# Causal attention of a fused transformer kernel: the order of TensorE's products within a unit, by the way they use the array

## What is computed

```python
q, k, v = x @ w_q[h].T, x @ w_k[h].T, x @ w_v[h].T      # per head h
scores  = q @ k.T / sqrt(64)                            # position i sees j <= i only
out     = concat_h(softmax(scores) @ v) @ w_o.T
x       = x + out
```

## Time and profile before

| | us |
|---|---|
| median of three runs | 2433.93 (2432.94 to 2435.12) |
| the profiled execution | 2433.29 |
| its span, first to last instruction | 2431.4 |
| TensorE busy, matmuls | 2165.6 (89%) |
| VectorE busy | 1550.0 (64%) |
| ScalarE busy | 1035.3 (43%) |
| mean granted TensorE clock | 0.947 of full speed |

### The profile page before, as it was taken

One profiled execution on the slowest core, in us unless ns is written; L12 is line 12 of the kernel. 1 busy time (PEld: TensorE's weight loads), 2 busy tenths in 40 slices (PEclk: granted clock), 3 DMA queues, 4 the chain that ended last, 5 costly groups with the idle time before them and its releaser, 6 DMA issues.

```text
span 2431.4 us, 39297 instructions
## 1 busy us (share of the span) xinstructions
PE 2165.6 (89%) x13553; PEld 1354.2 (56%) x13594; DVE 1550.0 (64%) x4432; ACT 1035.3 (43%) x1761; POOL 145.0 (6%) x271
## 2 busy tenths in 40 slices
PE   4569999996699989999999997999999599998698
PEld 3413333334577756566565665777766367775476
DVE  6798888857534346666666665444456735787776
ACT  2126666672234335555554553433333133343133
POOL 5011111115000000000000000000000000000000
PEclk9679999997799989999999998999999789999899
DMA  6010000000000000000000000000100000000000
GB/s 215 13 65 26 25 25 25 25 11 1 1 1 1 1 1 1 1 0 0 0 0 0 0 1 1 1 1 1 55 1 1 0 1 1 1 1 1 1 1 18
DMA packets 20863, 32.04 MB, mean 13 GB/s; under 512 B 5657, under 2 KB 12194, under 8 KB 19970
## 3 DMA queue, kind: packets, MB, share of 16 engines
q1 hardware_dynamic: 20018, 30.12, 3.6%
q10 hardware_dynamic: 720, 0.27, 0.1%
HBM read 25.80 MB, written 4.19 MB: 12 GB/s over the span
## 4 chain that ended last, share of the span: by engine, by line
PE 63%; DVE 9%; ACT 3%; issue 2%; ACTq 0%; DVEq 0%; POOL 0%; POOLq 0%
PE ps L408 19%; PE ps L393 18%; PE ps L604 6%; PE ps L638 5%; PE ps L621 3%; PE ps L588 3%; DVE x L819 1%; ACT arena L736 1%; PE ps L610 1%; PE ps L334 1%; DVE arena L801 1%; PE ps L901 1%; PE ps L256 1%; PE ps L650 1%; PE ps L1055 1%
## 5 line engine op out<-in xcount | busy, mean ns | idle before, releaser
L408 PEld LDWEIGHTS ps<-l_w,arena 128*128 128x128 f32 x4096 | 543.6, 194 | 262.2 <-issue 246.2
L408 PE MATMUL ps<-l_w,arena 128*128 128x128 f32 x4096 | 546.9, 277 | 12.1 <-DVE x L495 10.2
L393 PE MATMUL ps<-xnT,l_w 128*128 128x512 f32 x1024 | 537.8, 609 | 3.3 <-ACT xnT L264 3.3
L495 DVE SCALAR_TENSOR_TENSOR x<-ps,comb,x 128x128 f32<-128x128 f32 x768 | 216.4, 344 | 376.4 <-PE ps L408 374.5
L451 ACT ACTIVATE arena<-ps,l_b 128x512 f32<-128x512 f32 x384 | 263.6, 687 | 410.9 <-PE ps L393 410.8
L1962 DVE TENSOR_REDUCE arena<-ps 128x1 f32<-128x512 f32 x512 | 325.2, 685 | 34.2 <-PE ps L1747 32.2
L1890 ACT ACTIVATE arena<-ps 128x1024 f32<-128x1024 f32 x256 | 252.3, 1022 | 124.7 <-PE ps L1764 124.2
L801 DVE TENSOR_REDUCE arena<-ps 128x1 f32<-128x128 f32 (+7 forms) x256 | 179.0, 751 | 75.8 <-PE ps L610 74.5
L736 ACT ACTIVATE arena<-ps,arena 128x128 f32<-128x128 f32 (+7 forms) x256 | 186.8, 744 | 72.0 <-DVE arena L801 72.0
L1747 PE MATMUL ps<-arena 128*128 128x512 bf16 x480 | 173.6, 394 | 8.3 <-DVE arena L1962 6.0
L744 ACT ACTIVATE arena<-ps 128x512 f32<-128x512 f32 (+1 forms) x192 | 85.4, 489 | 211.6 <-PE ps L621 211.4
(11 more groups left out here) (319 smaller groups left out, 2036.6 us busy)
## 6 DMA issues: line engine op xcount, KB each, us to landing
arena<-s_parts_q SPq DMA_DIRECT2D x96, 48.0 KB
arena<-s_parts_k SPq DMA_DIRECT2D x96, 48.0 KB
l_w<-in_l_w SPq DMA_DIRECT2D x2, 2048.0 KB, 13.9
l_w<-in_l_w SPq DMA_DIRECT2D x4, 1024.0 KB, 12.3
s_parts_q<-arena SPq DMA_DIRECT2D x2, 768.0 KB, 4.3
s_parts_k<-arena SPq DMA_DIRECT2D x2, 768.0 KB, 5.2
arena<-arena SPq DMA_DIRECT2D x96, 2.0 KB
x<-in_x SPq DMA_DIRECT2D x4, 256.0 KB, 4.2
```

The lines of the kernel that those rows point to most:

```text
L393: pe.matmul(k.ps[:, n % 2, :], w.w1[:, e, f * P:(f + 1) * P], k.xnT[:, g * GW:(g + 1) * GW], start=True, stop=True).then_inc(s.hidden_mm.s ...
L408: ins = pe.matmul(k.ps[:, 2 + e % 4, j * P:(j + 1) * P], w.h[:, n % 2, j * P:(j + 1) * P], w.w2[:, e, f, :], start=(f == 0 and j == 0), st ...
L495: ins = dve.scalar_tensor_tensor(k.x[:, t, :], k.ps[:, 2 + e % 4, j * P:(j + 1) * P], k.comb[:, t, e:e + 1], k.x[:, t, :], ALU.mult, ALU.add)
```

## The change

TensorE's stream. Where there are projections, each unit now has exactly one, and it stands between the two `turn`s; `values` and `output` come after `turn(f, u, 1)`. The k projections move forward from behind `turn(f, u, 1)`. The waits are placed anew: `output` now waits for the copy of k out of bank 7, the q projection of u2 for `y_used` too, the v projection of u4 for `y_used` instead of a `kv_out`. ScalarE: `weights_out` is ahead of the exponentials in u2 too, and `q_copy` goes ahead of `o_copy`. VectorE: `kv_copy` of k moves ahead of `weights_out`, and `add` behind it.

```diff
                 turn(f, u, 0, begin)
+                if not end:
+                    if u == 0:
+                        pe.wait_ge(s.kv_out, 4 * f + 4)
+                        if b == 1:
+                            pe.wait_ge(s.slices, 2 * p + 4)
+                        project("q", 0, p + b, 1 - b, 7)
+                    if u == 1:
+                        pe.wait_ge(s.q_out, 2 * f + 3)
+                        project("k", 0, p + b, 1 - b, 7)
+                    if u == 2:
+                        pe.wait_ge(s.kv_out, 4 * f + 5)
+                        if not begin:
+                            pe.wait_ge(s.y_used, 4 * f - 1)
+                        project("q", 1, p + b, 1 - b, 7)
+                    if u == 3:
+                        pe.wait_ge(s.q_out, 2 * f + 4)
+                        project("k", 1, p + b, 1 - b, 7)
+                    if u == 4:
+                        pe.wait_ge(s.y_used, 4 * f + 1)
+                        project("v", 0, p + b, 1 - b, 7)
+                    if u == 5:
+                        pe.wait_ge(s.kv_out, 4 * f + 7)
+                        project("v", 1, p + b, 1 - b, 7)
+                turn(f, u, 1, begin)
                 if u == 0 and not begin:
                     values(f - 1, 1 - b, (6, 7))
                 if u == 1 and not begin:
-                    if not end:
-                        pe.wait_ge(s.q_out, 2 * f + 3)
+                    pe.wait_ge(s.kv_out, 4 * f + (4 if end else 5))
                     output(2 * f - 1, before)
                 if u == 2:
                     values(f, b, (2, 3), first=begin)
                 if u == 3:
-                    if not end:
-                        pe.wait_ge(s.q_out, 2 * f + 4)
+                    if end:
+                        pe.wait_ge(s.y_used, 4 * f - 1)
+                    else:
+                        pe.wait_ge(s.kv_out, 4 * f + 6)
                     output(2 * f, p)
                 if u == 4:
                     values(f, b, (4, 5))
-                if u == 0 and not end:
...
-                turn(f, u, 1, begin)
-                if u == 1 and not end:
-                    if begin:
-                        pe.wait_ge(s.q_out, 2 * f + 3)
-                    else:
-                        pe.wait_ge(s.y_used, 4 * f - 1)
-                    project("k", 0, p + b, 1 - b, 7)
-                if u == 3 and not end:
-                    pe.wait_ge(s.y_used, 4 * f + 1)
-                    project("k", 1, p + b, 1 - b, 7)
```

More of the change, by code:

```diff
@@ L757, in pair @@
             for u in range(U):
-                if u != 2:
-                    weights_out(f, u)
+                weights_out(f, u)
                 if u < U - 1:
@@ L763, in pair @@
                     exp(f + 1, 1 - b, 0)
-                if u == 2:
-                    weights_out(f, u)
+                if u in (0, 2) and not end:
+                    q_copy(f + 1, 1 - b, u // 2, 7)
                 if u == 0 and not begin:
@@ L769, in pair @@
                     o_copy(2 * f)
-                if u in (0, 2) and not end:
-                    q_copy(f + 1, 1 - b, u // 2, 7)
     q_copy(0, 0, 0, 2)
@@ L830, in pair @@
                     negmax(f + 1, 0)
+                if u in (4, 5) and not end:
+                    kv_copy("v", f + 1, 1 - b, u - 4, 7)
+                if u in (1, 3) and not end:
+                    kv_copy("k", f + 1, 1 - b, u // 2, 7)
+                weights_out(f, u)
                 if u == 1 and not begin:
@@ L834, in pair @@
                     add(f * 2, b * TB)
[L835 to L839, removed]
     for bank, what, g in ((3, "k", 0), (5, "k", 1), (6, "v", 0), (7, "v", 1)):
```

## The result

The changed kernel took 2423.0 us (median of 5 runs, 2418.4 to 2423.5), the kernel before 2433.9. The ratio is 0.9944, with a 95% interval of 0.9928 to 0.996: faster by 0.56%. The forecast was 2415.5, the range 2408 to 2426: right in sign and inside the range, with 11 us gained where 18.4 were forecast.

A forecast was written before the change was run, and what follows sets the result against it. TensorE's stream was taken as the bound. Per pass -1.30 - 1.79 + 1.80 = -1.3 us; fifteen passes -19.5, last pass +1.1, so 2433.9 - 18.4 = 2415.5 us, range 2408 to 2426.

The forecast's parts named there:

- What bounds: In a 37.6 us pass TensorE, busy 35.8 us, is the bound; only time leaving its stream shortens the pass.
- The changes removed: Seven of TensorE's 24 changes of array use per pass go, at 0.15 or 0.20 us each: 1.30 us saved.
- my first rival: At TensorE's removed changes of use, weight loads stay exposed, so the gain is only 6 us: 2428 us; chance 0.06.
- The waits removed: The k projections in u1 and u3 stop waiting for the addition to empty bank 7, and lose entries: 1.79 us.
- The waits added: TensorE waits for VectorE before u1's output, u2's values and u3's output: 2.10 us, or 1.80 net of exits.
- What stays at nothing: ScalarE's copies between the turns and its exponentials stay covered, with slack of about 0.1 and 0.4 us: no added wait.
- The last pass: Without projections, turns stand back to back in u0 to u4: 2.2 us lost, 1.1 saved on changes, so +1.1.
- The sum: Each pass 1.3 us shorter; fifteen passes -19.5, last pass +1.1: -18.4 us in all.
- its two unknowns: Scores' entry after output costing nothing (+6 us), and u2's VectorE chain off by 0.4 us either way (6 us).
- Rival 2: Before u2's values, VectorE's late addition delays TensorE one for one; taking twice its 2.59 us gives 2455 us; chance 0.05.

The follow-up runs named there:

- even units: The kernel before, with TensorE's new order in u0, u2 and u4 only and ScalarE's new order: 2428.3 us, ratio 0.9968.
- exchange of banks: The changed kernel with head 0's output in bank 6 and head 1's in bank 7, waits adjusted to match: 2405.7 us, 0.9876 of before.
- second timing: The unaltered changed kernel timed again against the kernel before, beside variants: 2422.4 us against 2435.7, ratio 0.9945.
- odd-units kernel: The changed kernel with TensorE's old order in u0, u2 and u4 and ScalarE's stream as before: 2429.3 us, ratio 0.9973.
- last-pass kernel: The changed kernel with values and output back between the two turns in the last pass alone: 2429.0 us, one execution.

## Why the prediction was right, and what it mis-sized

- *What bounds.* TensorE's stream, at a granted clock of 1.00 through the block. Every change to it showed in the time, pass by pass.
- *The changes removed, 1.30 us.* Right. The even units alone gave 0.58 for three (0.60 forecast); the other four, 0.70, were not timed by themselves, but the rows agree: a projection behind whole-array work takes 0.86 us, its pitch alone, and scores behind the output pay no entry (1.39 us against 1.49), the one that no row of before showed. The rule on which my first rival rested ("TensorE: Matmul & The Clock Gate", section "What overlaps and what doesn't", in the Trainium skill) did not decide here: projections of 128 rows behind transpositions of 128 rows went in 0.86 us, with no weight load in the open.
- *The waits removed, 1.79 us.* Right: no wait and no entry is left at line 588.
- *The waits added, 2.10 us.* This is the term that was mis-sized. By starts less pitch they are 0.19 (I said 0.17), 1.37 (1.2) and 0.71 or, in every other pass, 0.88 (0.73): 2.36 in the mean. With their exits taken off, 2.07 instead of 1.80. Of the 0.27, 0.18 is that the late semaphore was asked ahead of others in the loop: 0.10 in u2, and 0.17 in u3 of every other pass. The other 0.09, most of it in u2, I do not take apart.
- *What stays at nothing.* Right: ScalarE's copies were in time behind every projection, and its exponentials before u3's scores too.
- *The last pass, +1.1 us.* It was +1.3, nearly the number by luck and not for the reason. The `turn`s back to back, which I had at 2.2 less 1.1, cost 0.1: the last pass of the even units is 0.11 over before, and that of the exchange of banks, which has all of them but not u2's wait, is 0.12 over. u2's wait makes the other 1.20 (39.29 less 38.09), and I had left that out of this pass.
- *The sum.* -1.30 - 1.79 + 2.07 = -1.02; the passes gave -0.97, and the 0.05 between is not placed. 15 x 0.97 = 14.6 (14.9 between the marks in the table, since the first of the fifteen, 36.79 us before and 35.58 now, gained more), less 1.3: 13.6 us in the block, against 18.4. The second timing, with 11 runs of before, shows 13.3. The forecast's own bounds counted its two unknowns one at a time; both together would have reached 2427.5 us.
- *Rival 2* had the right place. Its break-even of 1.3 us was never reached, but the exchange of banks shows that the pass follows this wait nearly one for one, 1.20 us for 1.28. The addition itself did not get slower. One argument against this rival was misread: the addition with its reciprocal was not the same in u1 and u3. In u1 of the kernel before, VectorE's timeline has

```profile
1087.20 0.19 DVE L812 RECIPROCAL arena<-arena 128x8 f32<-128x8 f32 x1
1087.64 2.35 DVE L819 SCALAR_TENSOR_TENSOR x<-ps,arena,x 128x128 f32<-128x128 f32 x8 [0.25 <-PE ps L650]
```

and the copies behind it at 1089.91: 2.71 us, with a wait for the output in it, against 2.59 in u3. In the changed kernel it is 2.63 (1083.88 to 1086.51), so little hung on it.

## What to carry to other kernels

When a stream changes the way it uses the array, each change has a price that can be read from start to start, and putting like beside like saves it; but look first at what stood between the pieces that are brought together, since that work was cover for a wait. When a buffer that two consumers share makes one of them wait, see which half of the release each really needs: exchanging the two banks took back 1.20 us a pass of the wait that the reordering had made, more than the 0.97 of the reordering itself. (The exchange was not tried on the kernel before, whose values did not wait.) And put the semaphore that comes last at the end of the row of waits: in the loop that gave 0.18 us a pass, and still 0.08 with the banks exchanged.

## What the runs showed that I had not expected

The execution times of one and the same kernel spread over 5 us and more. In the two traces of the changed kernel, 2418.7 and 2422.4 us, none of the 3.6 us is in the block: the values of u0 start at 929.07 in the first and at 932.64 in the second, 3.57 later, and the passes are alike from there on. Two other kernels lie further apart. The scores of unit 1 in the first pass start as follows (timeline, TensorE), in the odd-units kernel and then in the last-pass kernel; all code ahead of them is the same:

```profile
887.61 3.36 PE L604 MATMUL ps<-arena 64*128 64x384 f32 x8 [0.69 <-ACT xnT L264]
```

```profile
899.24 3.36 PE L604 MATMUL ps<-arena 64*128 64x384 f32 x8 [0.69 <-ACT xnT L264]
```

That is 11.6 us apart after the same instructions, in single executions that ran on different chips (numbers 0 and 12). Between 550 and 650 us of the span, a stretch of the program with much waiting, their clocks differ:

```profile
550.00:650.00 100.00, 59.44 (x307) 46.93 (x307) 66.29 (x253) 20.74 (x30) 30.66 (x20) 0.73 0.00 1
```

```profile
550.00:650.00 100.00, 52.34 (x269) 43.13 (x269) 74.97 (x264) 15.51 (x22) 30.12 (x20) 0.68 0.00 1
```

The columns are those of the earlier trace rows; the granted clock is 0.73 in the first and 0.68 in the second, with more of the stretch at the lower of the two levels (1.2 GHz) in the later one. (The later one is also less far in its program there: 269 matmuls against 307.) Inside the block the clock was 1.00 in both, and the changed kernel's passes repeated to 0.02 us from one execution to another. Whether the clock or the chip explains the 11.6 us was not tested. For a change of half a per cent, the length of a pass in the trace told more than the medians.
